# The opening of a decoder layer rebuilt: state-space decays and input factors in PSUM, the first batch kept on chip, weight split and context statistics beside the preparation

## The reference, cut to what matters

```python
def _mamba(x, ...):                        # D_INNER 512, D_STATE 16
    xs, z = split(x @ W_in.T)              # convolution over 4 taps on xs, then silu
    dt, Bm, Cm = split(xs @ W_x.T)
    dt = softplus(dt @ W_dt.T + b_dt)
    dA = exp(dt[..., None] * A)            # A = -exp(A_log)
    dBx = dt[..., None] * Bm * xs[..., None]
    h = dA_t * h + dBx_t                   # for every position t, from h = 0
    y = sum over states of h * C_t, + xs * D
    return y * silu(z) @ W_out.T
x = layernorm(x + mamba(x))
x = layernorm(x + xattn(ctx, x))           # layer norms g1, b1 of ctx and g2, b2 of x; Wq, Wkv, Wout; 16 heads of 64
x = layernorm(x + ffn(x))                  # 8 experts, 2 chosen, and 2 shared
```

## Time and profile before

| | us |
|---|---|
| median of three runs | 3293.01 |
| lowest, highest | 3291.35, 3294.74 |
| profiled execution, its own time | 3294.52 |
| its span, first to last instruction | 3292.8 |
| mean granted TensorE clock | 0.945 |
| busy in the span: TensorE | 2997.8 (91%) |
| VectorE | 2038.2 (62%) |
| ScalarE | 1349.8 (41%) |
| GpSimd | 1087.5 (33%) |
| from the start to the first score product | 488.07 |

### The profile page before, as it was taken

One profiled execution on the slowest core, in us unless ns is written; L12 is line 12 of the kernel. 1 busy time (PEld: TensorE's weight loads), 2 busy tenths in 40 slices (PEclk: granted clock), 3 DMA queues, 4 the chain that ended last, 5 costly groups with the idle time before them and its releaser, 6 DMA issues. The chain is left out here.

```text
span 3292.8 us, 33914 instructions
## 1 busy us (share of the span) xinstructions
PE 2997.8 (91%) x11590; PEld 1863.3 (57%) x11590; DVE 2038.2 (62%) x3415; ACT 1349.8 (41%) x2310; POOL 1087.5 (33%) x824
## 2 busy tenths in 40 slices
PE   6634659999999999999999999999999999899997
PEld 3201335656566665656565665666566665586666
DVE  4667957777656767765677777565555545352225
ACT  4612315454435445453645455354434334321121
POOL 0057717575500567660036676100000000102213
PEclk8856759999999999999999999999999999799998
DMA  2342131121202111121122111110101100321112
GB/s 104 117 158 89 58 109 55 33 61 33 84 18 87 49 45 56 33 68 34 36 71 68 55 38 57 53 36 14 36 14 43 36 20 14 136 74 48 52 41 70
DMA packets 73182, 189.83 MB, mean 58 GB/s; under 512 B 8388, under 2 KB 42312, under 8 KB 64440
## 3 DMA queue, kind: packets, MB, share of 16 engines
q1 hardware_dynamic: 69176, 178.37, 17.8%
q0 software_dynamic: 3408, 9.31, 1.0%
q10 hardware_dynamic: 432, 0.01, 0.0%
HBM read 120.39 MB, written 32.64 MB: 46 GB/s over the span
## 5 line engine op out<-in xcount | busy, mean ns | idle before, releaser
L1293 PE MATMUL a_o<-a_p,a_vals 128*65 128x512 f32 (+1 forms) x2176 | 1113.5, 593 | 0.0
L900 ACT ACTIVATE a_p<-a_st 128x512 f32<-128x512 f32 (+1 forms) x1088 | 649.8, 597 | 1127.9 <-PE a_st L1281 1119.7
L1058 DVE TENSOR_REDUCE a_maxes<-a_mx 128x1 f32<-128x512 f32 x1024 | 683.0, 686 | 222.2 <-PE a_mx L1211 216.0
L1281 PE MATMUL a_st<-a_q,a_kone 65*128 65x512 f32 (+1 forms) x1088 | 430.6, 396 | 0.0
L790 POOL TENSOR_TENSOR a_shared<-a_shared,a_bc 128x512 f32<-128x512 f32 x192 | 249.2, 1298 | 387.2 <-DVE a_shared L992 387.2
L1293 PEld LDWEIGHTS a_o<-a_p,a_vals 128*65 128x65 f32 (+1 forms) x2176 | 284.3, 137 | 103.4 <-issue 1.8
L1280 PE MATMUL a_st<-a_q,a_keven 128*128 128x512 f32 (+1 forms) x544 | 326.0, 599 | 0.7 <-issue 0.7
L1280 PE MATMUL a_st<-a_q,a_kodd 128*128 128x512 f32 (+1 forms) x544 | 314.7, 579 | 0.0
L769 POOL TENSOR_TENSOR a_erstd<-a_emv,a_half 128x4 f32<-128x4 f32 x8 | 8.1, 1016 | 915.5 <-DVE a_emv L1084 915.5
L1211 PE MATMUL a_mx<-a_kodd,a_q 128*128 128x512 f32 x512 | 299.0, 599 | 8.4 <-DVE a_maxes L1058 7.3
L992 DVE TENSOR_TENSOR_SCAN a_shared<-a_shared 128x512 f32<-128x512 f32 x192 | 288.4, 1503 | 13.9 <-POOL a_shared L779 11.6
(11 more groups left out here) (244 smaller groups left out, 4543.9 us busy)
## 6 DMA issues: line engine op xcount, KB each, us to landing
a_bc<-m_kept_bc SPq DMA_DIRECT2D x64, 512.0 KB, 3.8
a_wt<-a_w_split SPq DMA_DIRECT2D x15, 1536.0 KB, 9.1
a_kone<-a_keven SPq DMA_DIRECT2D x32, 528.5 KB, 4.5
a_kone<-a_kodd SPq DMA_DIRECT2D x32, 528.5 KB, 4.3
e_wall<-in_w_t_dram SPq DMA_DIRECT2D x27, 512.0 KB, 9.5
a_shared<-in_ctx_dram SPq DMA_DIRECT2D x4, 1536.0 KB
a_w_split<-a_wt SPq DMA_DIRECT2D x4, 1536.0 KB, 8.6
e_y_dram<-e_y_row SPq DMA_DIRECT2D x39, 128.0 KB, 1.7
```

Of the source, the lines that this page charges most:

```text
L900: nc.scalar.activation(p[0:r, s % 4], st[0:r, s % 2], ACT.Exp, scale=SCALE).then_inc(exp_done, 1)
L1058: nc.vector.reduce_max(maxes[:, c, t:t + 1], mx[:, i % 2], AX_X).then_inc(mx_max, 1)
L1281: nc.tensor.matmul(st[0:r, s % 2], k_one[g % 2][0:DH + 1, kt * P:kt * P + r], qm[of(g)][0:DH + 1, :], start=False, stop=True).then_inc(st_ ...
L1293: nc.tensor.matmul(ps_o[0:DH + 1, g % 2], vals[0:r, kt * HG + j, :], p[0:r, s % 4], start=(kt == 0), stop=(kt == KT - 1)).then_inc(pv_done, 1)
```

## The change

The preparation moves into the attention's function (`prepare` in place of `mamba`), so that its tensors can be handed over: dt and du of the last batch stay in `carry`, y0 in `y`, z in the gate's buffer, and they are neither stored nor loaded for that batch. Its own `ident`, and the rates, norm weights, statistics and powers of the attention, are set in the preparation's block. The weight split is done there by GpSimd from three whole weights (1 MB each), with its four stores issued from GpSimd's queue, and the context's statistics by VectorE in the last turn. The same DRAM rows of B and C are loaded once for each pair of channel tiles, 32 loads in place of 16.

Units of the first batch now go pair by pair: `first_unit` gives all states for channel tiles 0 and 1, then for 2 and 3, so that two PSUM banks hold the sums in place of four. The freed banks and those of `a_mx` hold three decays and one copy of du. Unit u even: VectorE makes the input factor from that copy; u odd: GpSimd does, from `carry`. All products with C are GpSimd's. The scan stands two steps behind the inputs and C three, and the lists of ScalarE and VectorE place T, V and K a few steps later than TensorE's. The diff, cut to its core:

```diff
-def mamba(nc, x, w_in_t, conv_w, conv_b, w_x_t, w_dt_t, b_dt, a_log, d_skip, w_out_t, x1):
+def mamba(nc, *given):
+    KEPT["given"] = given
+
+def prepare(nc, ctx_rows, gammas, wq, wkv, w_dram, held):
+    carry, y0, zs, rows, wt, ident, a_neg, gb, stats, mv, rstd, half = held
+    dt, du = carry[:, 0], carry[:, 1]
+        raw = sb("m_raw", [P, 3, KD, H * DH])
...
         @block.sync
+            sp.dma_start(a_neg[:], a_log).then_inc(a_loaded, 16)
             for i in range(B + 1):
...
+                if i == 0:
+                    for j, src in enumerate((wq..., kv_src[:, :, 0:H * DH], kv_src[:, :, H * DH:2 * H * DH])):
+                        sp.dma_start(raw[:, j], src).then_inc(raw_loaded[j], 16)
+                if i == 1:
+                    for j, v in enumerate(gammas):
+                        sp.dma_start(gb[:, j], v).then_inc(gammas_loaded, 16)
+                    sp.dma_start(rows[:, 0:CTX_T - 1], ...).then_inc(rows_loaded, 16)
+                    sp.dma_start(rows[0:CL, CTX_T - 1], src[(CTX_T - 1) * P:LC]).then_inc(rows_loaded, 16)
-                if b >= 0:
+                if 0 <= b < B - 1:
                     sp.wait_ge(y0_ready, b + 1)
                     sp.dma_start(kept_y[b], ...)
-                if i < B:
+                if i < B - 1:
                     sp.dma_start(kept_z[i], ...)
-                if b >= 0:
+                if 0 <= b < B - 1:
                     sp.dma_start(kept_dtu[b, :, :, 0:S]..., dt)
                     sp.dma_start(kept_dtu[b, :, :, S:2 * S]..., du)
+            sp.wait_ge(gammas_loaded, 16 * 4)
+            sp.wait_ge(w_stored, 16 * NG)
...
         @block.gpsimd
+            for i in range(3 * NG):
+                n, which = NG - 1 - i // 3, i % 3
+                if i < 3:
+                    pool.wait_ge(raw_loaded[i], 16)
+                if which == 0 and i > 0:
+                    pool.wait_ge(w_stored, 16 * (i // 3))
+                part = raw[:, which, :, n * GW:(n + 1) * GW]
+                nc.gpsimd.tensor_copy(wt[:, 2 * which], part).then_inc(raw_high, 1)
+                pool.wait_ge(raw_high, i + 1)
+                nc.gpsimd.tensor_tensor(wt[:, 2 * which + 1], part, wt[:, 2 * which].bitcast(F32),
+                                        ALU.subtract).then_inc(raw_split, 1)
+                if which == 2:
+                    pool.wait_ge(raw_split, i + 1)
+                    pool.dma_start(w_dram[n], wt[:]...).then_inc(w_stored, 16)
+            pool.wait_ge(var_ready, 1)
+            nc.gpsimd.tensor_tensor(rstd[:, 0:CTX_T], mv[:, 0:CTX_T, 1], half[:, 0:CTX_T], ALU.pow).then_inc(rstd_made, 1)
...
         @block.vector
                 if b >= 0:
                     keep_xd(b)
+                if i == B:
+                    context_stats()
...
                     clip_dt(b)
+                if i == B:
+                    context_sums()
...
-FR = 3
+FD = 3
+FX = 4
 FS = 4
...
+LAG_H, LAG_C = 2, 3
+
+def first_unit(u):
+    pair, rest = divmod(u, 2 * NS)
+    return pair, rest // 2, 2 * pair + rest % 2
+
+def first(after_high, after_out):
+    early = []
+    for i in range(N_CTX + 3):
+        early += ([("N", 0, i)] if i < N_CTX else []) + ([("T", 0, i - 1)] if 0 < i <= N_CTX else [])
+        early += [("U", 0, i - 2)] if 1 < i <= N_CTX + 1 else []
+        early += [("V", 0, i - 3)] if 0 <= i - 3 < V_EARLY else []
+        early += [("K", 0, (i - 4) // 2)] if i in (4, 6, 8) else []
+    steps = [[] for _ in range(NU + 16)]
+    for u in range(NU):
+        steps[u].append(("D", 0, u))
+        steps[u + LAG_H].append(("H", 0, u))
+        steps[u + LAG_C].append(("C", 0, u))
+    for q in range(2):
+        steps[(q + 1) * 2 * NS + LAG_C].append(("Y", 0, q))
+    for i, what in enumerate(early):
+        at = i * (NU - 2) // len(early)
+        later = after_out if what[0] in "VK" else after_high if what[0] == "T" else 0
+        steps[at + later].append(what)
+    made = [x for one in steps for x in one]
...
+BEFORE, BEFORE_ACT, BEFORE_DVE = first(0, 0), first(1, 2), first(0, 3)
...
+        bc_first = [bc_early[:, 0:2], bc_early[:, 2:4], o_sb[:], shared[...]]
+        decay_first, dtu_bank = [mx[:, 0], mx[:, 1], ps_o[:, 1]], ps_o[:, 0]
...
         def sums(c):
-            return (st if c < 2 else ps_o)[:, c % 2]
+            return st[:, c % 2]
+
+        def p_of(k):
+            return carry[:, k // 2, 2 + k % 2]
...
+            def load_first(m):
+                pair, n = divmod(m, NS)
+                if m >= 4:
+                    wait_multiplied(sp, 0, 2 * (m - 4) + 1)
+                sp.dma_start(bc_first[m % 4]..., KEPT["bc"][BATCHES[0], n].partition_broadcast(P)).then_inc(...)
+            for m in range(4):
+                load_first(m)
+            sp.dma_start(w_out_first, ...)
             load_wo(0)
...
+            for m in range(4, 2 * NS):
+                load_first(m)
...
             def times_b(b, u):
+                if b == 0:
+                    if u % 2 == 1:
+                        wait_inputs_free(pool, 0, u, FX)
+                        wait_first_loaded(pool, u)
+                        nc.gpsimd.tensor_tensor(dbx_first[:, u % FX], dtu_of(0, c, 1), bc_first[u // 2 % 4][:, 0], ALU.mult)
+                    return
             def times_c(b, u):
+                if b == 0:
+                    pool.wait_ge(scanned, u + 1)
+                    nc.gpsimd.tensor_tensor(state_of(b, u), state_of(b, u), bc_first[u // 2 % 4][:, 1], ALU.mult)
+                    return
             def decays(b, u):
+                if b == 0:
+                    wait_inputs_free(act, 0, u, FD)
+                    nc.scalar.activation(decay_first[u % FD], dtu_of(0, c, 0), ACT.Exp, scale=a_neg[:, c, n:n + 1])
+                    if u == 2 * NS - 1:
+                        act.wait_ge(dbx_dve, NS)
+                        nc.scalar.activation(dtu_bank, carry[:, 1, 2], ACT.Copy).then_inc(dtu_turned, 1)
+                    return
+            def times_b_first(u):
+                if u % 2 == 0:
+                    dve.wait_ge(dtu_turned, u // (2 * NS) + 1)
+                    nc.vector.tensor_tensor(dbx_first[:, u % FX], dtu_bank, bc_first[u // 2 % 4][:, 0], ALU.mult)
             def scan(b, u):
-                if b == 0 and not on_pool(u):
-                    nc.vector.tensor_tensor(state_of(b, u), state_of(b, u), bc[:, i % 2, 1], ALU.mult)
+            def gate_first(q):
+                dve.wait_ge(summed, (q + 1) * 2 * NS)
+                for c in (2 * q, 2 * q + 1):
                     s = nc.vector.tensor_tensor(y[:, c], sums(c), y[:, c], ALU.add)
+                s.then_inc(sums_out, 1)
+                for c in (2 * q, 2 * q + 1):
                     nc.vector.tensor_tensor(y[:, c], y[:, c], gate[:, c], ALU.mult).then_inc(gated, 1)
             def sum_state(u):
+                if u == 2 * NS:
+                    pe.wait_ge(sums_out, 1)
```

More of the change, by code:

```diff
@@ L101, in mamba @@
         du_kept = sem("m_du_kept")
+        raw_loaded = [sem(f"m_raw_loaded{i}") for i in range(3)]
+        raw_high = sem("m_raw_high")
+        raw_split = sem("m_raw_split")
+        w_stored = sem("m_w_stored")
+        rows_loaded = sem("m_rows_loaded")
+        var_ready = sem("m_var_ready")
+        a_loaded = sem("m_a_loaded")
+        a_set = sem("m_a_set")
+        gammas_loaded = sem("m_gammas_loaded")
+        rstd_made = sem("m_rstd_made")
         block = ctx.enter_context(nc.Block())
@@ L156, in _ @@
             act.wait_ge(w_loaded, 16 * 7)
+            act.wait_ge(a_loaded, 16)
+            nc.scalar.activation(a_neg[:], a_neg[:], ACT.Exp).then_inc(a_set, 1)
             for i in range(B + 1):
@@ L407 @@
 BESIDE = [beside(g) for g in range(NH)]
-def first():
-    early = [("S", 0, t) for t in range(CTX_T)] + [("A", 0, i) for i in range(2)]
-    early += [("W", 0, i) for i in range(3 * NG)]
-    n_ctx = CTX_T // 2 + 1
-    for i in range(n_ctx + 1):
-        early += ([("N", 0, i)] if i < n_ctx else []) + ([("T", 0, i - 1)] if i > 0 else [])
-        early += [("U", 0, i - 2)] if i > 1 else []
-    early += [("U", 0, n_ctx - 1)]
-    early += [("V", 0, i) for i in range(V_EARLY)] + [("K", 0, i) for i in range(3)]
-    splits, others = [x for x in early if x[0] == "W"], [x for x in early if x[0] in "SANTU"]
-    head = []
-    for i, x in enumerate(others):
-        head += [x] + (splits[i // 2:i // 2 + 1] if i % 2 == 1 else [])
-    head += splits[len(others) // 2:]
-    early = head + [x for x in early if x[0] in "VK"]
-    made, done = [], 0
-    for u in range(NU + 3):
-        for kind, later in (("H", 1), ("D", 0), ("C", 2)):
-            if 0 <= u - later < NU:
-                made.append((kind, 0, u - later))
-        while done < len(early) and done * (NU - 4) < (u + 1) * len(early):
-            made.append(early[done])
-            done += 1
-    made += early[done:]
+LAG_H, LAG_C = 2, 3
@@ L816, in _ @@
                     times_c(*what[1:])
-                elif what[0] == "W":
```

(6 more changed lines are left out.)

300 lines of the change are left out of this document (125 added, 175 removed).

## The result

The kernel after takes 3172.22 us at the median of four runs (3170.8 to 3177.5), the kernel before 3293.88 beside it (3291.35 to 3298.04, four runs). The ratio is 0.9632, with a 95% interval of 0.962 to 0.9645: 121.7 us less, where 91.9 were forecast. The forecast of 3201 was 29 us too high; its range, 3168 to 3237, holds the result, 4 us above its lower end. The profiled execution has a span of 3170.9 us.

The account below looks back on a forecast made before the run. VectorE and GpSimd alternating in the scan stretch were taken as the bound. Terms +9 - 4.6 - 13.6 - 77.3 - 5.4 = -91.9 us took 3294.5 to 3202.6, 1.5 lower at the median: 3201, range 3168 to 3237.

Parts of the forecast that it names:

- the forecast's own case: Whole kernel: scan stretch of 150 us, total time of 3201 us, 91.9 us saved; chance 0.46.
- The rival of the scan that takes turns out of PSUM: Scan stretch: scans with decays in PSUM still alternate with GpSimd, 228 us, total time 3279 us; chance 0.06.
- The 150: Scan stretch after the change, taken midway between 130 and 171 us; saves 77.3 us.
- 171 from TensorE at 1.2 GHz: Scan stretch if TensorE sets the pace at 1.2 GHz: 171 us, total time 3222 us; chance 0.2.
- The floor: Scan stretch if VectorE and GpSimd interlock without loss: 130 us, with GpSimd priced at 130 and VectorE at 129.
- the second rival: Engines interlock well and splits miss the taps: stretch 130 us, splits cost 0, total time 3172 us; chance 0.2.
- the splits' price of the forecast: Preparation: GpSimd's 22.4 us of weight splits, times 0.45, delay VectorE's convolution taps; taken as +9 us.
- the 227: Scan stretch of the kernel before, 227.3 us, read as VectorE and GpSimd alternating, undisturbed work 232 us together.
- the mild and the slow rival: Split's stores from GpSimd's queue land late: mild, block end some 34 us late, 3235 us, chance 0.05; slow, 0.02.
- Preparation: Opening before the scans: splits beside the taps cost +9 us; statistics moved into a wait are free.
- Block end, first scan and last scan: Edges of the scan stretch: block end saves 4.6 us, up to first scan 13.6, behind last scan 5.4.
- "Nothing" for what follows: Projection, norms, latents, first maxima and attention behind the opening: order kept, no change in time.

Follow-up runs that it names:

- the doubled sums: Kernel after with each state sum made twice into the same bank on TensorE: 3179.1 us, scan stretch +2.7 us.
- The shortened sums: Kernel after with TensorE's sums of odd states, but the last, cut to 16 of 512 columns: 3173.71 us, scan stretch 128.2.
- The decays alone: Kernel before with only the first batch's decays written to two PSUM score banks, its order and split kept: 3258.12 us.
- both back in SBUF: Kernel after with the three decays and the copy of du put back in SBUF, order and moved work kept: 3244.13 us, stretch 196.7.

## Why the prediction was right, and where it was not

The result lies in the range and the direction and cause were right, but the forecast's own case, a stretch of 150 us and 3201, did not come.

**The mechanism, right.** VectorE and GpSimd take turns where VectorE reads two SBUF operands, and a decay in PSUM ends that: undisturbed scans in the kernel after, 51.5 us back with the decays in SBUF. The rival of the scan that takes turns out of PSUM falls by the 34 ns between the shortest and the longest scan.

**The 150, the step that failed.** It was put "midway between 130 and 171", with 171 from TensorE at 1.2 GHz. The floor was right: GpSimd and VectorE were priced at 130 and 129, and took 128.2. TensorE was mis-sized: a half-product of the sums was priced by its row, 0.59 us at the fast clock and 1.06 at the slow one, but takes 0.43 from start to start at the fast clock. The 128 of them are then 55 us and not 76, and by the doubled sums even twice as many nearly fit. At the slow clock a pair of halves on the kernel after's timeline is followed by TensorE's next row 1.86 us later, 0.93 for a half:

```profile
208.81 2.08 PE L1301 MATMUL a_st<-a_early,a_ident 128*128 128x512 f32 x2 [1.85 <-POOL a_early L842]
210.67 1.06 PE L1208 MATMUL a_ring<-a_ident,a_shared 128*128 128x128 f32 x4
```

That is 119, with the ring's 35 at most 154 and not 171. The clock did not stay low either, 0.86 on average. The shortened sums show directly that nothing of the stretch was TensorE's. This term, 22 us, is nearly all that the forecast fell short by in the stretch (99.1 against 77.3). The case that came true is the second rival's stretch (130) with the splits' price of the forecast; its 3172 was met by luck, because a preparation 5 us longer than it said was made up by 2 us in the stretch and 4 behind it.

**What the 227 consisted of, wrong though the sum fitted.** The prediction added all undisturbed work of both engines, 232, and read the stretch as pure alternation. By GpSimd's lines it was 126.6 of its own work, 43.4 of stretching (170.0 busy), and 57.3 standing still, of which 22.1 behind the split's stores and 29.0 behind scans. The turns were overpriced, since an instruction costs GpSimd 0.2 to 0.3 us less than it lasts, and nothing where GpSimd stands still anyway, and the waits were left out; the two errors met. In the kernel after the same account is 117.5 busy, nearly all of it undisturbed (94 x 1.24 = 116.6), and 10.7 idle: of the 99.1 us some 10 are less work on GpSimd, 42 less stretching, 47 less waiting. The decays alone saved 32.8 in the old list: 30.9 of stretching and 2.0 of waiting, with 12.5 of stretching left beside VectorE's products and 55.3 of waiting. In the new list they save 51.5, since there 55.2 of stretching hang on them. That the old list's waits hid a part of the turns is the likely reading; the products' share and that of the two decays in flight were not tried apart. Either part of the change brings something alone (32.8 and 30.6), and the 99.1 need both.

**The Trainium skill.** Its page SBUF — State Buffer (section "SBUF: two separate sides") says that of a VectorE operation with two SBUF inputs and a GpSimd one that reads SBUF, whichever starts first has the shared pair of ports "for the whole instruction; the other fully blocks". The direction agrees with every run here; as a price of the instruction's whole duration it is too high by the 0.2 to 0.3 us above. With the decays in SBUF 205 were expected and 180 measured, and of these 25 us the scans' lower price is 20: GpSimd was stretched by 55.2 and not by 74.9. On the "DVE blocks DMA" trap, the mild and the slow rival, that page speaks of VectorE's operations in a 2-port perf mode, which is narrower than the prediction's "an instruction that takes the shared port". No run here shows such a delay, but they hardly test it: the first store (26.4 to 32.0) ran beside SCALAR_TENSOR_TENSOR taps of two SBUF inputs, the third (53.6 to 59.0) met only the last TENSOR_SCALAR tap and then taps of that other kind, and the slowest, 8.3 us, lay where VectorE stood idle (39.2 to 47.5). The block's end waited for none of the stores. Why they landed sooner than from SP's queue is not shown; the other traffic was not the same.

**Preparation.** Forecast +9 (22.4 us of splits, 0.45 of them on the taps), measured +5.2. The splits alone cost 7 to 9, so this term was right within 2. Without them the last du comes 1.8 before that of the kernel before, which the prediction had not counted; 1.5 of it is there at the second batch's first tap (46.6 against 48.15), before any store of the last batch, and TensorE's projection just ahead takes 8.6 us there and 9.9 in the kernel before. The rest of its cause is open, and 1.8 is no more than equal preparations differ by. The spread was wrong: the disturbed taps are those of batches one and two, and the last two batches saw none. The prediction's own terms, 22.4 of splits and three stores of 8.6 between the groups, are 48 us and not 80; the last group's store was issued at 66.2, 48 behind the first cast. So the 0.45 came out about right with two batches of taps in 48 us in place of three in 80.

**The edges.** Block end, first scan and last scan came within 0.3 us of their terms; the context statistics, 4.33 + 0.95 us in the last batch, ran where VectorE had waited for the delta products, and the double loading of B and C rows delayed nothing in the stretch. "Nothing" for what follows was 4.2 us too little: 1.0 is the projection, the other 3.2 are spread over 2800 us, 0.1%, and no cause of them is shown. They may be scatter: the same part takes 2805.1 with the decays in SBUF and 2801.2 with both back in SBUF, though neither touches it.

## What to carry to other kernels

Where VectorE's long instructions read two SBUF operands beside a busy GpSimd, put one of them in PSUM: a 512-column scan then costs GpSimd nothing where it had cost about 0.9 us. Before pricing such a gain, split the stretch of the engine that is held up into own work, stretching and standing still; the middle part is what the turns cost first of all, and what stands still in the same list (a single buffer behind a store, a scan) has to be moved away too before the whole gain comes through. Price TensorE from start to start of neighbouring rows at a known clock, never by the durations' sum, and let side work on GpSimd start when VectorE's instructions that take turns with it are done.

## What the runs showed of the hardware that was not expected

- A scan of 1.19 us cost GpSimd's product beside it 0.86 to 0.91, a VectorE product of 0.66 cost it 0.36 to 0.47: the taking of turns is not end to end.
- A TENSOR_SCALAR of VectorE, with one SBUF tensor read, takes turns with GpSimd too: four taps lasted 3.03 and 2.60 us beside the splits, 1.67 without them.
- A matmul row of 128 x 512 fp32 lasts 0.59 us and the next starts after 0.43: rows overlap by a quarter.
- The split's four stores of 1.5 MB from GpSimd's queue landed in 5.5 us at the median (5.4 to 8.3), sooner than from SP's queue beside the scans (8.6).
- TensorE's granted clock over the stretch was 0.69 with shortened, 0.86 with whole and 0.97 with doubled sums, while the stretch stayed within 128 and 131 us.
